# Vision tower on one core: layer norms by logarithm and exponential, folds inside the norms, pair blocks inside the last attention

## Chip, core and metric

The kernel runs on one core of a Trainium2 chip. The metric is the device time of one launch in microseconds. All data is fp32, apart from two 0/1 matrices in bf16.

## The reference

What is computed, cut to its order:

```python
h = tok(x)                          # 128 images -> 64 patches + class token, 128 wide; times pos_embed
h = h + attn0(layernorm(h))         # 8 heads; scores below the 64th best of 65 dropped;
                                    # sum over i=1..3 of gelu(alpha_i) * attn^i v
h = h + mlp0(layernorm(h))          # 64 experts' places with capacity 128, top 2, one shared MLP
h = h + attn1(layernorm(h))         # softmax attention, and a fixed distance matrix on a 4th projection
h = h + mlp1(layernorm(h))          # 8 experts, top 2 of them for each token, weights by softmax
layernorm(x) = (x - mean(x)) / sqrt(var(x) + 1e-5)      # over the 128 features
```

## The kernel before

The residual stream `h` and the normalised stream `xn` lie in SBUF whole, features on partitions, 8320 tokens in the free axis (128 images of 65). `vit_tower` (from L2202) calls one function for each stage, and each stage is a block of its own: all engines meet at its end, and each engine runs its own list of instructions in between, tied to the others by semaphores alone.

- `patch_embed` (L92) streams the images in sixteen chunks and fills `h`. ScalarE issues the small loads; GpSimd has nothing to do.
- `fold_first` (L2107) makes small folded matrices for the first attention: gelu of the alphas, their sum, `center_w` = identity - 1/128, the value weights turned on TensorE (4 transposes), scaled, and multiplied with the output weights (4 products). `fold_second` (L2167) does the like for the second layer.
- `layer_norm` (L205) is called three times (tags a0, f0, a1). It goes over 10 groups of 832 tokens. TensorE: `center` (2 matmuls of 416 columns with `center_w`, three PSUM banks in turn, L253), `variance` (four 32-row means of the squares, L260), `spread` (four matmuls that spread the inverse deviation over 128 rows into four banks, L269), in the order center(g), variance(g-1), spread(g-2). ScalarE: two copies out of PSUM (L297), square root (L289), square (L305). VectorE: reciprocal (L315) and the multiplication into `xn` (L320). The four banks of `spread` aren't doubled: spread(g) waits for normalise(g-1).
- `attention` (L394) is called twice. It goes over 64 pairs of images in a software pipeline; steps 64 to 79 are the drain. In the second call it carries `Routing` as well: for each batch of 4 tiles of 128 tokens (the sixteenth and last has 5) it turns the finished rows of `h` (`turn_rows`, L1549), computes the second norm's mean and deviation (logarithm L921, exponential L926), picks two of eight experts, ranks tokens by expert pair, and GpSimd scatters rows to the DRAM tensor `pair_rows` (`send`, L650). Before that, `complete_rows` (L637) adds the turned rows of `h` to the bias sums that TensorE made (`weigh_biases`, L1598) and ScalarE copied (`copy_biases`, L896 and L897). `normalise_rows` is L885. At the end VectorE computes a table of blocks (`find_blocks`), and SyncE clears all used semaphores in a block of its own (L1645).
- `pair_blocks` (L1895) loads 93 blocks of 128 rows from `pair_rows` (L1970), runs two experts on each (up L2010, down L2020) and scatters the results to `out` (L1990). Ahead of its first load it makes a tile of pad rows (L1985) and stores it (L1956).

## Time and profile before

| | us |
|---|---|
| three runs | 1830.36, 1833.38, 1837.22 |
| median | 1833.38 |
| profiled execution, time | 1838.73 |
| profiled execution, span from first to last instruction | 1836.9 |
| TensorE busy in the span | 1662.0 (90%) |
| VectorE, ScalarE, GpSimd busy | 1092.3, 872.8, 777.7 |

The page's picture of the span, in 40 slices of 45.9 us, digits in tenths of a slice:

```profile
## 2 busy tenths in 40 slices
PE   8999998899999999987899989999999998459997
...
PEclk9999998999999999999699989999999999679999
```

Stages by their first instruction, in us from the span's start: patches 0, first fold 268.8, norm a0 274.3, first attention 309.8, norm f0 840.9, routed MLP 876.4, second fold 1044.6, norm a1 1048.0, second attention 1081.6, semaphores cleared from 1614.1, pair blocks 1621.6, end 1836.9. A row of a timeline gives the start, the duration and, in brackets, how long the engine sat idle before it and what ended that. PE is TensorE, DVE VectorE, ACT ScalarE, POOL GpSimd, SP SyncE, and a q behind a name is that engine's sequencer. One fp32 matmul is two instructions in a row's count. The clock column is the granted TensorE clock, 1.0 for 2.4 GHz and 0.5 for 1.2 GHz.

### The profile page before, as it was taken

How to read it: one execution, taken by the hardware profiler on the slowest of the kernel's cores; microseconds unless marked ns; L12 is line 12 of the kernel's file. 1: busy time of each engine (PE TensorE's matmuls, PEld its weight loads, DVE VectorE, ACT ScalarE, POOL GpSimd, SP SyncE). 2: the span in 40 equal slices, each digit the busy share in tenths (PEclk: the TensorE clock that was granted, in tenths of full speed). 3: DMA queues.
4: the chain of work that ended last, by engine and by line, in shares of the span. 5: the costliest groups of instructions: out<-in, count | busy, mean ns of one | idle time of the engine just before them, and what ended most of it. 6: DMA issues, size and time to landing. Idle time of an engine off the chain costs nothing. (4 is left out here: it accounts for less than half of the span.)

```text
span 1836.9 us, 61849 instructions
## 1 busy us (share of the span) xinstructions
PE 1662.0 (90%) x24177; PEld 1227.1 (67%) x24177; DVE 1092.3 (59%) x3338; ACT 872.8 (48%) x2369; POOL 777.7 (42%) x925
## 2 busy tenths in 40 slices
PE   8999998899999999987899989999999998459997
PEld 3444444677777777763877647777777777358997
DVE  0000015888878888874666555766666666537765
ACT  0000006666666656545444455665656565236653
POOL 0000000788888878870011113355545454514444
PEclk9999998999999999999699989999999999679999
DMA  9877730000000000003000000000000000124422
GB/s 374 319 313 313 298 122 1 3 3 4 3 3 4 3 3 4 3 4 103 1 1 1 1 1 3 2 20 20 20 19 20 20 22 17 48 78 119 124 75 62
DMA packets 47216, 117.17 MB, mean 64 GB/s; under 512 B 10732, under 2 KB 29471, under 8 KB 46973
## 3 DMA queue, kind: packets, MB, share of 16 engines
q1 hardware_dynamic: 39198, 99.25, 15.0%
q0 software_dynamic: 6096, 12.94, 2.0%
q8 instruction: 191, 3.13, 0.7%
q10 hardware_dynamic: 1678, 1.43, 0.2%
q14 instruction: 53, 0.43, 0.1%
HBM read 96.80 MB, written 18.61 MB: 63 GB/s over the span
## 5 line engine op out<-in xcount | busy, mean ns | idle before, releaser
L1361 PE MATMUL ps<-xn,s_a_wqkv 128*128 128x260 f32 x1024 | 302.8, 414 | 29.1 <-ACT qk_a L768 22.5
L170 PE MATMUL ps<-x_chunk,s_w_tok 128*128 128x512 f32 x576 | 252.2, 599 | 6.7 <-DMA x_chunk<-in_x_main 6.7
L1361 PEld LDWEIGHTS ps<-xn,s_a_wqkv 128*128 128x128 f32 x1024 | 170.8, 192 | 105.3 <-ACT qk_a L768 71.3
L170 PEld LDWEIGHTS ps<-x_chunk,s_w_tok 128*128 128x128 f32 x576 | 109.8, 192 | 147.8 <-issue 147.8
L940 ACT ACTIVATE e_a<-e_a 128x585 f32<-128x585 f32 (+1 forms) x128 | 85.1, 665 | 167.2 <-DVE e_a L1248 96.6
L197 DVE SCALAR_TENSOR_TENSOR h<-ps,s_b_tok,s_pos 128x512 f32 (+1 forms) x16 | 11.3, 746 | 249.4 <-PE ps L178 249.4
L724 POOL TENSOR_TENSOR prob_a<-e_a,inv_sum_a 128x512 f32<-128x512 f32 x64 | 67.0, 1047 | 206.6 <-issue 111.0
L614 POOL MEMSET cls_queries_a<- 128x1040 f32 x2 | 1.9, 966 | 346.6 <-POOLq L221 346.6
L1239 DVE TENSOR_REDUCE neg_max_a<-ps 128x8 f32<-128x520 f32 x128 | 89.3, 697 | 99.1 <-PE ps L1339 99.1
L1445 PE MATMUL ps<-s_a_wqkv,xn_pair_a 128*64 128x256 f32 x1024 | 138.5, 389 | 4.5 <-ACT weightsT_m L875 2.8
L1990 POOL DMA_INDIRECT out<-block_out_m,block_m x93 | 92.1, 990 | 114.9 <-DVE block_out_m L2093 74.0
L2126 ACT ACT_TABLE_LOAD x1 | 1.3, 1283 | 268.8 <-PEq L103 268.8
L708 POOL TENSOR_TENSOR kept_a<-e_a,keep_a 128x585 f32<-128x585 f32 x64 | 87.3, 1364 | 89.8 <-issue 76.8
L1401 PE MATMUL ps<-horner_a,probT_a 64*64 64x64 f32 x2048 | 109.5, 219 | 6.0 <-issue 5.7
L1401 PE MATMUL ps<-dv_a,probT_a 64*64 64x64 f32 x2048 | 107.4, 219 | 5.8 <-issue 2.8
L768 ACT ACTIVATE qk_a<-ps 128x260 f32<-128x260 f32 x256 | 99.1, 387 | 27.9 <-PE ps L1361 19.6
L780 ACT ACTIVATE resT_a<-ps 128x260 f32<-128x260 f32 x256 | 84.5, 383 | 58.4 <-PE ps L1378 35.8
L1411 PE MATMUL ps<-probT_a,horner_a 64*64 64x65 f32 x2048 | 109.8, 224 | 1.6 <-DVE horner_a L985 1.5
L1892 POOL TENSOR_TENSOR h<-h,mlp_gated 128x320 f32<-128x320 f32 x26 | 22.4, 863 | 186.6 <-DVE mlp_gated L1872 186.6
L1411 PE MATMUL ps<-probT_a,cls_values_a 64*64 64x1 f32 x2048 | 92.1, 187 | 6.3 <-issue 6.3
L1339 PE MATMUL ps<-qk_a 64*64 64x65 f32 x4096 | 91.8, 224 | 3.4 <-issue 3.4
L1248 DVE TENSOR_TENSOR e_a<-ps,neg_max_a 128x520 f32<-128x520 f32 x128 | 89.7, 701 | 6.0
(284 smaller groups left out, 4356.5 us busy)
## 6 DMA issues: line engine op xcount, KB each, us to landing
x_chunk<-in_x_main SPq DMA_DIRECT2D x96, 768.0 KB, 8.4
block_m<-pair_rows SPq DMA_DIRECT2D x93, 130.0 KB
pair_rows<-pad_rows_m SPq DMA_DIRECT2D x29, 130.0 KB
s_f_all<-in_f_w SPq DMA_DIRECT2D x2, 1024.0 KB
x_ends<-in_x_tail SPq DMA_DIRECT2D x16, 96.0 KB, 10.7
out<-block_out_m,block_m POOLq DMA_INDIRECT x93
s_w_tok<-in_w_tok SPq DMA_DIRECT2D x6, 192.0 KB, 6.9
pair_rows<-rows_m,slot_i_m POOLq DMA_INDIRECT x65
```

Of the source, the lines that this page charges most:

```text
L170: last = nc.tensor.matmul(ps[:, bank, :], w_tok[:, k, :], xb[:, s, k, :], start=(k == 0), stop=False)
L708: nc.gpsimd.tensor_tensor(columns(kept, t.even), columns(e_of(t), t.even), columns(keep, t.even), ALU.mult).then_inc(kept_done, 1)
L768: nc.scalar.activation(qk[:, (t.j // 2) % 2, c, :], ps[:, QK_BANK[i], 0:QUAD], ACT.Identity if bias is not None else ACT.Copy, bias=bias[: ...
L940: nc.scalar.activation(columns(e_of(t), t.even), columns(e_of(t), t.even), ACT.Exp, scale=-SCALE)\
L1239: last = nc.vector.tensor_reduce(neg_max[:, :, 0:CH], score(), AX.X, ALU.min)
L1248: last = nc.vector.tensor_tensor(e_of(t)[:, :, 0:CH], score(), over_keys(neg_max[:, :, 0:CH]), ALU.subtract)
L1339: last = nc.tensor.matmul(ps[i * PATCHES:(i + 1) * PATCHES, b, c * SEQ:(c + 1) * SEQ], qk[rows, sl, c, t0 + 1:t0 + SEQ], qk[rows, sl, CH + ...
L1361: nc.tensor.matmul(ps[:, QK_BANK[i], 0:QUAD], w_qkv[:, c * P:(c + 1) * P], xn[:, t.h * QUAD:(t.h + 1) * QUAD], start=True, stop=True).then ...
L1401: last = nc.tensor.matmul(ps[rows, 2 + n, col:col + DH], pt[rows, k, c, i, 1:SEQ], values[rows, i, c, :], start=True, stop=True)
L1411: last = nc.tensor.matmul(ps[other, R_BANK[i], c * SEQ:c * SEQ + cols], values[rows, (t.j - 6) % 2, i, c, :], pt[rows, k, c, i, 0:cols], s ...
L1445: last = nc.tensor.matmul(ps[b * DH:(b + 1) * DH, V_BANK, i * CH * DH:(i + 1) * CH * DH] .rearrange("p (c d) -> p c d", c=CH), xs[:, k, i ...
L1990: nc.gpsimd.indirect_dma_start(out[:, :], bass.IndirectOffsetOnAxis(ap=blk[:, s % RB, NAME:NAME + 1].bitcast(I32), axis=0), ys[:, s % RY, ...
```

## The change

1. `layer_norm`: VectorE copies the centered values out of PSUM. ScalarE squares, then takes the logarithm of variance + eps and the exponential of -0.5 times that, which is the inverse deviation; no reciprocal is left, and the dummy square root at the head becomes an explicit choice of table set. VectorE normalises two groups behind its copies.
2. `fold_first` and `fold_second` are gone. The constants are made in `patch_embed` (ScalarE and GpSimd); the transposes and products stand in the norms' tails (`Fold`, passed to the norms a0 and a1).
3. `attention`: GpSimd runs `complete_rows` behind `add_cls`. For the last batch it isn't run; TensorE adds the rows of `h` in PSUM by five products with the identity. In the drain ScalarE normalises rows one step earlier.
4. `pair_blocks` becomes the class `PairBlocks`. Its engine parts follow the attention's in the same block, with the same instructions in the same order, and its buffers lie in `xn` and `h`. The pad rows are made at the attention's head. SyncE waits for the block table and for all scattered rows, then loads. The block that clears semaphores is left out behind the second attention.

```diff
--- before.py
+++ after.py
@@ patch_embed @@
+            nc.scalar.activation(consts.alphas[:, :, :], consts.alpha_raw, ACT.Gelu).then_inc(gelu_done, 1)
+            act.wait_ge(gelu_done, 1)
+
+        @block.gpsimd
+        def _(pool):
+            nc.gpsimd.memset(consts.mean_w[:, :], 1.0 / D).then_inc(means_set, 1)
+            nc.gpsimd.memset(consts.spread_w[:, :], 1.0 / 32).then_inc(folded, 1)
+            nc.gpsimd.memset(consts.dist_pair[:, :, :], 0.0).then_inc(folded, 1)
+            pool.wait_ge(means_set, 1)
+            pool.wait_ge(later_loaded, 16 * len(later_loads))
+            nc.gpsimd.tensor_tensor(consts.center_w[:, :], consts.ident[:, :], consts.mean_w[:, :], ALU.subtract)\
+                .then_inc(folded, 1)
+            nc.gpsimd.tensor_scalar(consts.neg_b_q[:, :], consts.b_q, -1.0, None, ALU.mult).then_inc(folded, 1)
+            pool.wait_ge(gelu_done, 1)
+            nc.gpsimd.tensor_tensor(consts.asum[:, :], consts.alphas[:, :, 0], consts.alphas[:, :, 1], ALU.add)\
+                .then_inc(asum_done, 1)
+            pool.wait_ge(asum_done, 1)
+            nc.gpsimd.tensor_tensor(consts.asum[:, :], consts.asum[:, :], consts.alphas[:, :, 2], ALU.add)\
+                .then_inc(asum_done, 1)
+            pool.wait_ge(asum_done, 2)
+            nc.gpsimd.tensor_tensor(consts.abv[:, :], consts.asum[:, :], consts.bv_col, ALU.mult).then_inc(folded, 1)
+            pool.wait_ge(folded, 5)
...
@@ layer_norm, TensorE @@
+            def turn_values():
+                pe.wait_ge(copied, 2 * groups)
+                for c in range(CH):
+                    last = nc.tensor.transpose(ps[:, 2, c * P:(c + 1) * P], fold.w_v[:, c * P:(c + 1) * P],
+                                               fold.ident[:, :])
+                last.then_inc(wvt_ps, 1)
+                for c in range(CH):
+                    last = nc.tensor.matmul(ps[:, 1, 0:fold.wide], fold.left(c), fold.right(c),
+                                            start=(c == 0), stop=(c == CH - 1))
+                last.then_inc(wide_ps, 1)
+
+            def fold_values():
+                pe.wait_ge(wvt_sb, 1)
+                for c in range(CH):
+                    last = nc.tensor.matmul(ps[:, 0, 0:D], wv_t[:, c, :], fold.w_out[:, c, :],
+                                            start=(c == 0), stop=(c == CH - 1))
+                last.then_inc(wcls_ps, 1)
+
             for g in range(groups + 2):
                 if g < groups:
                     center(g)
@@ -277,54 +337,72 @@
                     variance(g - 1)
                 if g >= 2:
                     spread(g - 2)
+                if fold and g == groups:
+                    turn_values()
+            if fold:
+                fold_values()
...
@@ layer_norm, ScalarE and VectorE @@
+            nc.scalar.preload_act_table_set("natural_log_exp_and_others")
             act.wait_ge(eps_set, 1)
-            nc.scalar.activation(warm[:, :], eps[:, :], ACT.Sqrt).then_inc(warmed, 1)
-
-            def deviation(g):
+
+            def square(g):
+                act.wait_ge(copied, 2 * g + 2)
+                since(act, var_ps, g - 1)
+                nc.scalar.activation(sq[:, g % 2], xc[:, g % SX], ACT.Square).then_inc(squared, 1)
+
+            def inverse(g):
                 act.wait_ge(var_ps, g + 1)
-                since(act, rstd_done, g - 1)
-                nc.scalar.activation(sd[:, g % 2, :], ps[:, 3, 0:n], ACT.Sqrt, bias=eps[:, 0:1])\
-                    .then_inc(sd_done, 1)
+                nc.scalar.activation(log_var[:, g % 2, :], ps[:, 3, 0:n], ACT.Ln, bias=eps[:, 0:1])\
+                    .then_inc(log_done, 1)
+                act.wait_ge(log_done, g + 1)
+                since(act, spread_ps, g - 1)
+                nc.scalar.activation(rstd[:, g % 2, :], log_var[:, g % 2, :], ACT.Exp, scale=-0.5)\
+                    .then_inc(rstd_done, 1)
 
             for g in range(groups + 1):
                 if g < groups:
-                    since(act, normed, g - SX + 1)
-                    for q in (2 * g, 2 * g + 1):
-                        act.wait_ge(center_ps, q + 1)
-                        nc.scalar.activation(xc[:, g % SX, 2 * (q % 2):2 * (q % 2) + 2, :],
-                                             ps[:, q % 3, 0:half].rearrange("p (i n) -> p i n", n=n),
-                                             ACT.Copy).then_inc(copied, 1)
+                    square(g)
                 if g >= 1:
-                    deviation(g - 1)
-                if g < groups:
-                    act.wait_ge(copied, 2 * g + 2)
-                    since(act, var_ps, g - 1)
-                    nc.scalar.activation(sq[:, g % 2], xc[:, g % SX], ACT.Square).then_inc(squared, 1)
-            act.wait_ge(warmed, 1)
+                    inverse(g - 1)
 
         @block.vector
         def _(dve):
             nc.vector.memset(eps[:, :], EPS).then_inc(eps_set, 1)
 
-            def inverse(g):
-                dve.wait_ge(sd_done, g + 1)
-                since(dve, spread_ps, g - 1)
-                nc.vector.reciprocal(rstd[:, g % 2, :], sd[:, g % 2, :]).then_inc(rstd_done, 1)
+            def copy(g):
+                since(dve, squared, g - SX + 1)
+                since(dve, normed, g - SX + 1)
+                for q in (2 * g, 2 * g + 1):
+                    dve.wait_ge(center_ps, q + 1)
+                    nc.vector.tensor_copy(xc[:, g % SX, 2 * (q % 2):2 * (q % 2) + 2, :],
+                                          ps[:, q % 3, 0:half].rearrange("p (i n) -> p i n", n=n)).then_inc(copied, 1)
 
             def normalise(g):
-                dve.wait_ge(copied, 2 * g + 2)
                 dve.wait_ge(spread_ps, g + 1)
                 nc.vector.tensor_tensor(xn[:, g * Q * n:(g + 1) * Q * n].rearrange("p (i n) -> p i n", n=n),
                                         xc[:, g % SX], ps[:, 4:4 + Q, 0:n], ALU.mult).then_inc(normed, 1)
 
-            for g in range(groups + 1):
+            for g in range(groups + 2):
                 if g < groups:
-                    inverse(g)
-                if g >= 1:
-                    normalise(g - 1)
+                    copy(g)
+                if g >= 2:
+                    normalise(g - 2)
+                if fold and g == groups:
+                    dve.wait_ge(wvt_ps, 1)
+                    turned = ps[:, 2, :].rearrange("p (c f) -> p c f", c=CH)
+                    if fold.scale is None:
+                        nc.vector.tensor_copy(wv_t[:, :, :], turned).then_inc(wvt_sb, 1)
+                    else:
+                        nc.vector.tensor_tensor(wv_t[:, :, :], turned, fold.scale.unsqueeze(2).to_broadcast([P, CH, D]),
+                                                ALU.mult).then_inc(wvt_sb, 1)
+            if fold:
+                dve.wait_ge(wide_ps, 1)
+                fold.finish(ps[:, 1, 0:fold.wide]).then_inc(wcls_sb, 1)
+                dve.wait_ge(wcls_ps, 1)
+                nc.vector.tensor_copy(fold.w_cls[:, :], ps[:, 0, 0:D]).then_inc(wcls_sb, 1)
+                dve.wait_ge(wcls_sb, 2)
...
@@ attention, SyncE and GpSimd @@
+                blocks.store_spare_rows(sp)
+                sp.wait_ge(table_done, 1)
+                for i in range(2):
+                    sp.wait_ge(sent[i], 16 * sum(route.size(k) for k in range(i, route.batches, 2)))
+                blocks.sync(sp)
...
                 k, par = at
-                n = route.size(k)
+                if isinstance(k, int) and k == LAST:
+                    return
                 upto(pool, b2_sb, k + 1, route.batches)
-                nc.gpsimd.tensor_tensor(rows[:, par, 0:n, D:2 * D], rows[:, par, 0:n, D:2 * D],
-                                        turned[:, par, 0:n, 0:D], ALU.add).then_inc(added, 1)
+                nc.gpsimd.tensor_tensor(rows[:, par, 0:route.BATCH, D:2 * D], rows[:, par, 0:route.BATCH, D:2 * D],
+                                        turned[:, par, 0:route.BATCH, 0:D], ALU.add).then_inc(added, 1)
...
+                if isinstance(k, int) and k == LAST:
+                    pool.wait_ge(b2_sb, k + 1)
+                else:
+                    upto(pool, added, k + 1, LAST)
...
@@ attention, step of GpSimd @@
-                if route and t.j % 4 == 0:
-                    complete_rows(t)
...
                 if t.even != masked and t.has(depth):
                     add_cls(t)
+                if route and t.j % 4 == 0:
+                    complete_rows(t)
...
@@ attention, ScalarE @@
+                ends = t.fixed and t.s >= pairs
                 if t.j % 4 == 0:
                     copy_turned(t, 0)
+                    if ends:
+                        normalise_rows(t)
...
@@ attention, TensorE and the end @@
                 for i in range(n):
+                    whole_rows = n > route.BATCH
                     last = nc.tensor.matmul(biases_at(i), wtt[0:n * E1, :], b2_diag[0:n * E1, i * D:(i + 1) * D],
-                                            start=True, stop=True)
+                                            start=True, stop=not whole_rows)
+                    if whole_rows:
+                        first = (k * route.BATCH + i) * P
+                        last = nc.tensor.matmul(biases_at(i), h[:, first:first + P], ident[:, :],
+                                                start=False, stop=True)
...
+                blocks.tensor(pe)
 
         stage_block.close()
+        if route:
+            return
```

## Rows read from the trace of the kernel before

**Rows 1.** Busy time by stretch: stretch, length, each engine's busy us, clock, DMA, GB/s.

```profile
1048.00:1081.60 33.60, 27.52 (x200) 12.02 (x200) 23.41 (x21) 23.39 (x42) 0.00 (x0) 0.94 0.00 1
1110.00:1555.00 445.00, 416.88 (x7061) 342.35 (x7060) 296.20 (x1001) 269.16 (x782) 214.87 (x300) 1.00 0.05 17
...
1624.80:1837.00 212.20, 189.83 (x1581) 181.09 (x1581) 141.51 (x435) 116.00 (x343) 92.08 (x93) 0.96 0.34 98
...
877.00:903.00 26.00, 26.00 (x124) 26.00 (x124) 13.75 (x68) 10.43 (x24) 0.00 (x0) 0.50 0.01 1
```

**Rows 2.** Timeline, two groups of a norm: start, duration, engine, line, operation, idle before.

```profile
1062.71 0.63 PE L269 MATMUL ps<-rstd_a,spread_w 32*128 32x208 f32 x8 [0.32 <-DVE xn L320]
...
1063.28 1.66 PE L253 MATMUL ps<-h,center_w 128*128 128x416 f32 x4
...
1064.30 0.96 DVE L320 TENSOR_TENSOR xn<-centered_a,ps 128x832 f32<-128x832 f32 x1
...
1064.87 0.56 PE L260 MATMUL ps<-squared_a,mean_w 128*32 128x208 f32 x8
...
1065.50 0.43 ACT L289 ACTIVATE deviation_a<-ps,eps_a 128x208 f32<-128x208 f32 x1
1065.83 0.89 ACT L305 ACTIVATE squared_a<-centered_a 128x832 f32<-128x832 f32 x1
1065.97 1.45 DVE L315 RECIPROCAL rstd_a<-deviation_a 128x208 f32<-128x208 f32 x1 [0.70 <-ACT deviation_a L289]
...
1065.97 1.66 PE L253 MATMUL ps<-h,center_w 128*128 128x416 f32 x4
```

**Rows 3.** Timeline, tail of the same norm: its last center and its last normalise.

```profile
1071.70 1.66 PE L253 MATMUL ps<-h,center_w 128*128 128x416 f32 x4
...
1080.31 1.02 DVE L320 TENSOR_TENSOR xn<-centered_a,ps 128x832 f32<-128x832 f32 x1 [1.35 <-PE ps L269]
```

**Rows 4.** VectorE's copies out of PSUM by line: min, median, max ns.

```profile
L1001 DVE COPY probT_a<-ps x64: 680/692/693, 1101.8 to 1568.1; 128x512 f32<-128x512 f32 x64
...
L2196 DVE COPY w_dist<-ps x1: 292/292/292, 1046.2 to 1046.2; 128x128 f32<-128x128 f32 x1
```

**Rows 5.** Timeline: both folds, the norms' first centers, the first attention's first projections.

```profile
268.83 0.63 PE L2132 MATMUL ps<-s_ident,s_a_wqkv 128*128 128x128 f32 x4 [1.92 <-PEq L103]
...
274.32 5.24 PE L253 MATMUL ps<-h,center_w 128*128 128x416 f32 x8 [0.86 <-PEq L2115]
...
311.02 6.84 PE L1361 MATMUL ps<-xn,s_a_wqkv 128*128 128x260 f32 x16 [0.46 <-ACT cls_out_a L749]
...
1044.64 0.63 PE L2179 MATMUL ps<-s_ident,s_a_wqkv 128*128 128x128 f32 x4 [1.88 <-PEq L1669]
...
1048.08 3.03 PE L253 MATMUL ps<-h,center_w 128*128 128x416 f32 x8 [0.87 <-PEq L2170]
```

**Rows 6.** Timeline, end of the last attention: rows of the last two batches.

```profile
1581.42 1.24 PE L1549 MATMUL ps<-turn_gate_m,h 128*128 128x136 f32 x4 [2.79 <-POOL h L679]
...
1592.61 2.02 ACT L885 ACTIVATE rows_m<-turned_m,row_shift_m,row_rstd_m 128x128 f32<-128x128 f32 x5
...
1594.99 2.47 PE L1598 MATMUL ps<-s_a_wqkv,weightsT_m 40*128 40x128 f32 x10 [1.66 <-issue]
...
1598.35 1.53 POOL L637 TENSOR_TENSOR rows_m<-rows_m,turned_m 128x640 f32<-128x640 f32 x1 [2.76 <-ACT rows_m L897]
...
1600.78 0.99 POOL L650 DMA_INDIRECT pair_rows<-rows_m,slot_i_m  x1 [0.90 <-POOL rows_m L637]
```

**Rows 7.** Queue drains by line (ns; first to last start); first load, last store.

```profile
L1644 POOLq DRAIN  x2: 727/3050/5374, 834.6 to 1608.6; - x2
...
L1913 POOLq DRAIN  x1: 9327/9327/9327, 1827.4 to 1827.4; - x1
...
1624.88 1.49 SPq L1970 DMA_DIRECT2D block_m<-pair_rows  x2
...
1828.06 0.98 POOL L1990 DMA_INDIRECT out<-block_out_m,block_m  x1 [0.30 <-issue]
```

More of the change, by code:

```diff
@@ L740, in _ @@
             if route:
-                for i in range(2):
-                    pool.wait_ge(sent[i], 16 * sum(route.size(k) for k in range(i, route.batches, 2)))
+                blocks.gpsimd(pool)
         @block.scalar
@@ new lines, in gpsimd @@
+    def gpsimd(self, pool):
+        nc, blk, ys, RB, RY = self.nc, self.blk, self.ys, self.RB, self.RY
+        for s in range(self.count):
+            pool.wait_ge(self.y_done, s + 1)
+            nc.gpsimd.indirect_dma_start(
+                self.out[:, :],
+                bass.IndirectOffsetOnAxis(ap=blk[:, s % RB, self.NAME:self.NAME + 1].bitcast(mybir.dt.int32), axis=0),
+                ys[:, s % RY, :], None, bounds_check=self.tokens - 1, oob_is_err=False)\
+                .then_inc(self.stored[s % RY], 16)
```

503 lines of the change are left out of this document (231 added, 272 removed).

## Prediction

> **What bounds the kernel now.** I read the page's slices first, then busy time by stretch, then the timeline at every seam. In the attention of the second layer TensorE is busy 416.9 of 445 us at the full clock, and in the pair blocks 189.8 of 212.2 us [rows 1]. There only fewer matmuls would help, and the diff removes none. What is loose lies between the stages and in the three layer norms: one norm takes 33.6 us, with TensorE busy 27.5, VectorE 23.4 and ScalarE 23.4 [rows 1]. So I cost each norm, the two fold blocks, the end of the last attention and the hole behind it.
>
> **Folds taken out of their own blocks.** The first fold runs from 268.83 to the norm's first matmul at 274.32, 5.5 us; the second from 1044.64 to 1048.08, 3.4 us [rows 5]. Both stretches go. The constants (gelu, alpha sums, center_w) move to ScalarE and GpSimd inside the patch block, which have nothing to compute for some 165 us after their loads; cover enough, and the gelu's table load is in it. What remains of a fold moves to the tail of its norm, below.
>
> **Steady part of a norm.** Groups of 832 tokens start alternately 3.04 and 2.69 us apart. The group from 1063.28 has no wait: center until 1064.87 (1.59), then variance and spread until the next center at 1065.97 (1.10), in sum 2.69; in the other the spread waits 0.32 for VectorE's normalise, which stands behind a 1.45 us reciprocal [rows 2]. After the change VectorE has two copies and the normalise. A copy of 128x512 from PSUM takes 0.69 and one of 128x128 takes 0.29, so 416 columns take about 0.59 [rows 4]: 2 x 0.59 + 0.96 = 2.14 us. ScalarE has square 0.89, logarithm and exponential. A logarithm of this shape is not in the trace; I price both like the square root, 0.43 [rows 2], so 1.75 us, against bounds of 0.2 (half of it) and 0.9 (the square) each; even at the upper bound the sum is 2.69. So TensorE sets 2.69. Seven groups from the third to the tenth go from a mean of 2.87 to 2.69, -1.2; the first variance comes some 0.3 later, as both first copies now run one behind the other ahead of the square. Net -0.9 for each of three norms. The table load at a norm's head (1.28 us) still lies beside the first centers and copies.
>
> **Tail of a norm.** From the last center (1071.70) to the end of the last normalise (1081.33) pass 9.63 us [rows 3], a chain of reciprocals and normalises through one set of PSUM banks. After: copies done at +2.3, square at +3.2, last variance at +3.9, exponential at +5.0; meanwhile the ninth normalise ends at +5.9, the last spread at +6.6, the last normalise at +7.7. That is -2.0 in the middle norm. In the outer two the fold's transposes and the four wide products stand ahead of the last spread (0.6 + 1.0 us on TensorE, 0.69 on VectorE), so it starts 0.4 later; behind it come four products, 1.1, and a copy of 0.29. I end at +8.7, -0.9 each.
>
> **Clock of the first norm.** Its first eight matmul instructions take 5.24 us, those of the second layer's norm 3.03 [rows 5]: the first stretch ran at the 1.2 GHz level, after a fold in which TensorE was mostly idle, the other at 2.4 GHz. With the fold gone TensorE goes from the patch products over a 1.9 us hole straight into centers. I take the upper level: -1.9, since filling hides part of the 2.2. The tail with its fold leaves hardly a hole ahead of the attention, whose first sixteen projection instructions took 6.84 us at the lower level [rows 5]; at the upper they could take 3.4, and as ScalarE has to empty the two banks in turn I take 4.5: -2.3, between 0 and -3.4. In the last attention a DMA of 3 us gates the start, so nothing is gained there. If the clock falls anyway, these 4.2 us are lost. The Trainium skill, page "TensorE: Matmul & The Clock Gate" (Part 1), says that the gate follows how busy the array was lately, and that it takes sustained work to get the full rate back; by that rule too the outcome hangs on the hole ahead of the norm.
>
> **Order in the last attention.** GpSimd's row sum now stands behind the class-token adds. In the loop both wait for things that come at the same times as before and GpSimd has slack, so 0. In the drain TensorE waits 2.79 us for h behind that sum [rows 6]; the next limit, ScalarE's first copy, comes 1.6 earlier than 1581.42, so 1.6 is gained. Row normalising, 2.02 us on ScalarE ahead of the last weight copy [rows 6], moves into an idle stretch in both last batches: 0.4 and 1.1. Together the last bias products start 3.1 earlier. Five more products there, at the 0.49 of one of the five now in 2.47 us [rows 6], add 2.4; GpSimd's 1.53 us sum leaves; and the first row is sent after 0.4 where it took 0.9 behind that sum [rows 6]. Sum: -3.1 + 2.4 - 1.5 - 0.4 = -2.6, give or take 1.5: the same move in the third last batch puts 1.6 us of ScalarE ahead of evictions of one step and takes it from ahead of those of the next, and I count that as nothing. VectorE's block table is ready 2 us earlier as well and isn't last.
>
> **The hole behind it.** Now: last row sent 1606.84, its landing seen by GpSimd by 1608.4, GpSimd's queue drains 5.37 us from 1608.6, then 118 semaphores are cleared until 1621.5, pads are made and stored, and the first block load issues at 1624.88 [rows 7]: 18.0 us. After: SyncE waits for the landing (1.6) and reads its row register (1.0), then loads: 2.6. So -15.4. Weight fetches of VectorE and ScalarE need only the table and lie in that wait. GpSimd's two pad memsets, 0.4 us, and the spare-row store move to the attention's head, where SyncE is idle and ScalarE waits for the iotas behind them; the 3 us DMA gates there.
>
> **A cost that comes back.** The drain isn't free elsewhere. 5.374 us for 65 indirect DMAs is 82.7 ns each. The kernel's last drain ends at 1836.7, 7.69 us after the last indirect issue ends at 1829.04, with 93 DMAs since the drain before: 82.7 ns each again [rows 7]. I take it as a cost per indirect DMA since the last drain. In one block there are 158, so 13.07 us at the end: +5.4.
>
> **Sum.** First norm: -5.5 - 0.9 - 0.9 - 1.9 - 2.3 = -11.5. Middle: -0.9 - 2.0 = -2.9. Last: -3.4 - 0.9 - 0.9 = -5.2. End of attention and hole: -2.6 - 15.4 + 5.4 = -12.6. In all -32.2 on the profiled execution of 1838.7 us (span 1836.9), so 1806.5 there. That execution lay 5.3 above the median of the runs, 1833.4; the prediction is 1801.2.
>
> **Rivals.**
> - *The drain is no more than a constant*, or cleared records are taken up while GpSimd idles: then nothing comes back. For: GpSimd is busy 92 of 212 us in the blocks [rows 1]. Against: two drains with the same 82.7. 1801.2 - 5.4 = 1796.
> - *The norms gain nothing inside*, from a latency that I don't see (copies late for the square), and the clock falls ahead of the first norm: 6.0, 2.9 and 1.8 of the three sums go, 10.7 in all: 1812.
> - *The router keeps the full clock.* Behind the middle norm TensorE runs 26 us without a hole at the lower level [rows 1]. A shorter tail might keep the upper one; then VectorE, 13.75 us of work, is next: -12, 1789. Against: TensorE is still mostly idle in that tail, which has no fold to fill it.
> - *Slower: table loads between the functions.* If square, logarithm and exponential didn't stay in one table set, each group would pay 1.28 us twice. It decides from 0.94 us on ScalarE per group (2.69 - 1.75). ScalarE's group would be 1.75 + 2.57 = 4.3, 1.6 over TensorE's, 30 times: +48.6, 1850. Against: the last attention runs logarithm and exponential at once one behind the other with identity and copy, with one load at its head. The Trainium skill ("ScalarE: Activation LUTs", Table sets) says that one named set holds exp and ln, and that cheap functions are in every set; for square this trace shows it only beside the root.
>
> **How the numbers follow.** Forecast 0.61, no drain paid again 0.12, norms flat 0.14, router at full clock 0.07, table loads 0.04, something unseen that eats most of it 0.02. The forecast's own range is 1797 to 1806 (the 4.2 us of the clock, logarithm and copy prices, 1 or 2 us in the drain). 1792 to 1812 leaves out the router, the loads and the unseen. A measurement of this kernel tells about 0.5%, 9 us, from no change: faster 0.91, same 0.05, slower 0.04.
>
> **What would show it.** Centers 2.69 apart in all three norms, with no table load between; the first eight at 3.0 us in the first norm; no TensorE instruction of a fold outside a norm; the first block load 2.6 us behind the last row's issue; no drain there, and a last drain of about 13 us behind the last store. Wrong if groups come at 2.9 or more, or if GpSimd stalls among its stores once more than 93 are out since the last drain.

## The result and the profile after

The changed kernel takes 1800.1 us (median of four runs, 1796.46 to 1800.6); the kernel before, timed beside it, 1831.9 (1824.47 to 1837.22). The ratio is 0.983, with an interval from 0.980 to 0.986: 31.8 us less, where the prediction had 32.2 less and 1801.2. A second comparison, with both kernels timed on one chip, gave 1815.2 against 1847.1, 0.985 (0.982 to 0.987), again 31.9 less. The number was right. Its terms were not all: one cost that I added hardly exists, and another, of about the same size, I did not see.

The first rows are busy time by stretch of the changed kernel's first profiled execution (time 1796.46 us, span 1794.6): stretch, its length, busy us and instructions of TensorE, of its weight loads, of VectorE, ScalarE and GpSimd, then the granted clock, the DMA share and GB/s. They are the first norm, the router, the middle of the last attention and the pair blocks.

```profile
268.00:299.10 31.10, 28.92 (x220) 13.96 (x221) 22.60 (x34) 17.35 (x31) 0.03 (x1) 1.00 0.01 2
866.00:894.00 28.00, 27.89 (x131) 27.92 (x132) 14.88 (x74) 9.17 (x23) 0.00 (x0) 0.50 0.00 1
1110.00:1555.00 445.00, 413.08 (x7049) 341.71 (x7048) 305.56 (x1070) 270.25 (x791) 222.96 (x306) 1.00 0.05 18
1582.00:1794.60 212.60, 190.46 (x1581) 181.38 (x1581) 141.15 (x435) 115.56 (x343) 92.89 (x93) 0.96 0.34 98
```

Beside [rows 1]: a norm with its fold inside now takes 31.1 us, with TensorE busy 28.9 of them; a norm alone took 33.6 with 27.5. The router is still at 0.50, that is 1.2 GHz, and the two long stages are what they were.

One whole group of the middle norm, from the timeline (start, duration, engine, line, operation, idle time before):

```profile
850.06 1.67 PE L295 MATMUL ps<-h,center_w 128*128 128x416 f32 x4
850.20 1.02 DVE L384 TENSOR_TENSOR xn<-centered_f,ps 128x832 f32<-128x832 f32 x1 [0.49 <-PE ps L311]
...
850.54 0.42 ACT L357 ACTIVATE log_variance_f<-ps,eps_f 128x208 f32<-128x208 f32 x1
...
850.99 0.38 ACT L361 ACTIVATE rstd_f<-log_variance_f 128x208 f32<-128x208 f32 x1
851.16 1.19 DVE L379 COPY centered_f<-ps 128x416 f32<-128x416 f32 x2
...
851.65 0.56 PE L302 MATMUL ps<-squared_f,mean_w 128*32 128x208 f32 x8
...
852.14 0.63 PE L311 MATMUL ps<-rstd_f,spread_w 32*128 32x208 f32 x8
852.39 0.90 ACT L353 ACTIVATE squared_f<-centered_f 128x832 f32<-128x832 f32 x1 [1.02 <-DVE centered_f L379]
...
852.71 1.66 PE L295 MATMUL ps<-h,center_w 128*128 128x416 f32 x4
```

Centers come 2.65 apart, group after group, with no waiting TensorE; [rows 2] had 2.69 and 3.04 in turn. VectorE works 2.21 and ScalarE 1.70 of the 2.65. No table load stands between square, logarithm and exponential: with that the slower rival falls. The Trainium skill ("ScalarE: Activation LUTs", Table sets) says that one set has logarithm and exponential together; the trace agrees, and shows square under that set too, with one load of 1.28 us at each norm's head.

The seams of the same execution. TensorE at the first norm's head, in its folded tail and at the attention's start:

```profile
268.05 3.03 PE L295 MATMUL ps<-h,center_w 128*128 128x416 f32 x8 [1.93 <-PEq L111]
...
297.07 1.16 PE L329 MATMUL ps<-s_a_wout,wvT_a 128*128 128x128 f32 x8
...
300.24 3.69 PE L1457 MATMUL ps<-xn,s_a_wqkv 128*128 128x260 f32 x12 [0.46 <-ACT cls_out_a L837]
...
304.30 1.14 PE L1457 MATMUL ps<-xn,s_a_wqkv 128*128 128x260 f32 x4 [0.36 <-ACT qk_a L856]
```

The first eight center instructions take 3.03 where [rows 5] had 5.24, and the sixteen projections are through after 5.2 us where they took 6.84. Last come the old hole and the end: the last row's issue, the first block load, the first product behind it, the last store, and the queue drains by line (min/median/max ns, first to last start).

```profile
1578.49 0.96 POOL L739 DMA_INDIRECT pair_rows<-rows_m,slot_i_m  x1 [0.30 <-issue]
...
1581.99 1.48 SPq L2090 DMA_DIRECT2D xn<-pair_rows  x2
...
1584.03 0.48 PE L2119 MATMUL ps<-s_ident,xn 128*128 128x128 f32 x1 [11.66 <-DMA xn<-pair_rows]
...
1785.32 0.98 POOL L2106 DMA_INDIRECT out<-h,xn  x1 [0.31 <-issue]
...
L1746 POOLq DRAIN  x2: 728/5235/9742, 827.8 to 1784.6; - x2
```

From the end of the last row's issue (1579.45) to the load are 2.5 us; in [rows 7] there are 18.0. The last drain ends at 1794.39, 8.08 behind the last store's issue (1786.31), where it was 7.66 before.

Reading such seams off ten of the profiled executions gives this table, in us; the columns are the two profiles of either kernel and one of each experiment that follows. The stages run from the last patch product to the first scores, from there to the last class-token add, from the middle norm's first matmul to the router's, on to the last expert add, to the second attention's first scores, through 64 steps to the last pair's probabilities, to the last row's issue, to the first block load, to the last store's issue, and to the end.

| | before, second profile | order only | changed, first profile | order back | before, first profile | norms only | folds out | own block | changed, second profile | eight small matmuls |
|---|---|---|---|---|---|---|---|---|---|---|
| first norm with fold | 53.9 | 53.9 | 40.5 | 41.5 | 52.1 | 50.6 | 50.6 | 40.5 | 40.5 | 41.6 |
| first attention | 518.5 | 522.0 | 522.5 | 525.0 | 516.8 | 518.2 | 520.6 | 522.3 | 525.2 | 524.8 |
| middle norm | 35.0 | 35.0 | 31.9 | 31.9 | 35.5 | 31.9 | 32.3 | 31.9 | 31.9 | 32.0 |
| router, experts | 169.6 | 169.6 | 169.7 | 169.7 | 167.9 | 169.6 | 169.6 | 169.8 | 169.8 | 156.7 |
| fold, last norm | 49.4 | 48.5 | 42.9 | 42.9 | 48.9 | 45.8 | 45.1 | 42.8 | 42.9 | 42.6 |
| last attention | 459.5 | 459.5 | 459.4 | 459.5 | 469.0 | 469.2 | 469.0 | 468.9 | 468.8 | 469.0 |
| its end | 44.8 | 42.9 | 41.3 | 43.2 | 44.7 | 44.9 | 45.9 | 44.5 | 44.5 | 44.6 |
| hole | 18.2 | 18.5 | 2.5 | 2.5 | 18.0 | 18.0 | 2.5 | 8.3 | 2.5 | 2.6 |
| pair blocks | 206.2 | 199.8 | 204.4 | 205.8 | 204.2 | 205.1 | 208.5 | 202.3 | 205.0 | 202.9 |
| last drain | 7.9 | 7.9 | 8.3 | 8.3 | 7.9 | 7.9 | 8.3 | 7.9 | 8.3 | 8.3 |
| span | 1833.6 | 1828.0 | 1794.6 | 1801.9 | 1836.9 | 1831.7 | 1823.1 | 1810.4 | 1810.0 | 1796.9 |

The reader is to see two families in the row of the last attention: 459.4 to 459.5, and 468.8 to 469.2, whatever the kernel. The two profiles that I compared first lie in different ones. That gives a span difference of 42.3 us, of which 9.6 has nothing to do with the change. Within one family the spans differ by 39.0 and 26.9 us, on either side of the 32 of the timed runs, so single executions scatter by several us. From the stage differences I had expected 40 us and a ratio of 0.978 for the second comparison; it gave 0.985.

### The profile page after: what moved, and what is told of

It reads as the page before. It is cut to its first block and busy times, and to the rows that moved or that the text cites. A ratio compares the mean times of both kernels' runs of the same rounds, so it can differ in the third digit from the quotient of the medians.

```text
span 1794.6 us, 61648 instructions
## 1 busy us (share of the span) xinstructions
PE 1654.6 (92%) x24187; PEld 1223.5 (68%) x24187; DVE 1083.3 (60%) x3361; ACT 849.9 (47%) x2334; POOL 778.0 (43%) x932
## 3 DMA queue, kind: packets, MB, share of 16 engines
q8 instruction: 191, 3.13, 0.7%
## 5 line engine op out<-in xcount | busy, mean ns | idle before, releaser
L2106 POOL DMA_INDIRECT out<-h,xn x93 | 92.9, 999 | 114.0 <-DVE h L2219 107.4
L1541 PEld LDWEIGHTS ps<-s_a_wqkv,xn_pair_a 128*64 128x64 f32 x1024 | 67.5, 137 | 36.4 <-issue 17.2
```

The source lines that it names most:

```text
L1541: last = nc.tensor.matmul(ps[b * DH:(b + 1) * DH, V_BANK, i * CH * DH:(i + 1) * CH * DH] .rearrange("p (c d) -> p c d", c=CH), xs[:, k, i ...
L2106: nc.gpsimd.indirect_dma_start(self.out[:, :], bass.IndirectOffsetOnAxis(ap=blk[:, s % RB, self.NAME:self.NAME + 1].bitcast(mybir.dt.int32 ...
```

## The experiments

**The kernel before once more, and the order of GpSimd's row sum.** On that first comparison the last attention had become 9.6 us shorter, in steps of 0.8 per period of four pairs, and the only edit in its loop is the order of two things on GpSimd. Either that order costs 0.8 per period (theory A), or it is something of the execution (theory B, TensorE's instruction supply). I ran the kernel before again, the changed kernel with the order undone, and the kernel before with that edit alone. The edit, as in the second of them:

```diff
             def step(t):
+                if route and t.j % 4 == 0:
+                    complete_rows(t)
                 if t.has(1):
...
                 if t.even != masked and t.has(depth):
                     add_cls(t)
-                if route and t.j % 4 == 0:
-                    complete_rows(t)
```

> The kernel before, unchanged, so that a second profiled execution of it stands beside the first. The first one was at 1838.7 us, above all timed runs (1824.5 to 1837.2). In the last attention, whose four-pair period is 31.2 us there and 30.4 after the change, each theory says what a second look shows. Theory A (the order of GpSimd's row sum costs 0.8 us per period, 12 times): the period is 31.2 again, since the order is in the program. Theory B (TensorE's instruction supply ran dry once per period in that one execution): the period can be 30.4 here, and the span some 9 us shorter. The ratio to the kernel before is 1.000 by both.

> The changed kernel with one edit: in the last attention's loop GpSimd's row sum stands ahead of the class-token adds again, as before. TensorE's program is untouched. Theory A (that order cost 12 x 0.8 us in the loop, besides 1.6 in the drain): the period goes from 30.4 to 31.2 us and the whole time from 1800 to some 1811. My forecast's reading (GpSimd has slack in the loop, the order counts in the drain alone): 1801 to 1802, period 30.4. Theory B (instruction supply of TensorE): same as the forecast's reading.

> The kernel before with that one edit of the change: GpSimd's row sum behind the class-token adds. Theory A: 1832 less 11 = 1821. The forecast's reading: 1832 less 1.6 at the most, 1830. Theory B: no change beyond the scatter of the kernel before.

Measured: 1830.2 against 1829.5 for the kernel before (ratio 1.000), 1803.6 for the order undone (0.986, 0.983 to 0.988), 1827.4 for the order alone (1.000, 0.998 to 1.003). The last attention takes 459.5 in all three: theory A is wrong. The order counts only at the attention's end, where both kernels show 1.9 us: 44.8 to 42.9 with the edit alone, 41.3 to 43.2 with it undone, against 1.6 in the forecast. In the timeline of GpSimd with the order alone, the row sum of the third last batch now stands behind the add that it used to hold up:

```profile
1572.56 0.73 POOL L679 TENSOR_TENSOR h<-h,cls_terms_a 128x260 f32<-128x260 f32 x1 [4.07 <-DVE h L1020]
1574.66 1.26 POOL L637 TENSOR_TENSOR rows_m<-rows_m,turned_m 128x512 f32<-128x512 f32 x1 [1.37 <-ACT rows_m L897]
```

1.9 us is a tenth of a per cent, too little for whole runs to tell; only the seams show it. Theory B holds no better as it stands. The slow loops appeared in every kernel of two later sets of runs, each set on one chip, and in none of this one. So the family goes with the chip that a set runs on, or with something else of its time; the runs don't tell which. From 1200 to 1500 us TensorE is idle on "issue" for 3.2 us in the first profile of the kernel before and for none in the second; that is less than half of the 0.8 us in each of some ten periods, and what the rest is stays open.

**What a drain of GpSimd's queue costs.** The last drain was to be 13.07 us and is 8.08 behind the last issue. A kernel with nothing but row scatters measures the law by itself. Its body, once for each count:

```diff
+        with nc.Block() as sixty_five:
+            @sixty_five.gpsimd
+            def _(pool):
+                send_rows(nc, pool, region, rows, place, sems[3], 42, 65)
```

> Leaves out the whole model: the output is zeros. GpSimd alone sends rows to DRAM by indirect DMAs of 128 rows of 1040 bytes, as the last attention does, 2, 8, 32, 65, 158 and three times 65 of them, each batch in a block of its own, so that GpSimd's queue drains at each end; each DMA waits for the landing of the one two before it. In the sixth batch GpSimd waits for the last landing before the block ends, in the seventh it then idles some 20 us more, in the eighth it computes some 5 us between two DMAs. The forecast's rule (82.7 ns for each indirect DMA since the last drain): 0.2, 0.7, 2.6, 5.4, 13.1, 5.4, 5.4 and 5.4 us. Rival (a constant after the last issue, some 7 to 8 us less what has passed by the drain's start, whatever the count): about 7 in the first five, 5 in the sixth, near 0 in the seventh, 7 in the eighth. A third reading (cost by the number of DMAs up to a limit, or of those not yet taken up): 158 at once gives far more than 8, and the slow eighth batch gives less than the fourth.

The drains of the batches, by line, as above, without the second:

```profile
L89 POOLq DRAIN  x1: 3893/3893/3893, 26.1 to 26.1; - x1
...
L97 POOLq DRAIN  x1: 4181/4181/4181, 89.2 to 89.2; - x1
L101 POOLq DRAIN  x1: 6556/6556/6556, 189.5 to 189.5; - x1
L105 POOLq DRAIN  x1: 5004/5004/5004, 428.3 to 428.3; - x1
L109 POOLq DRAIN  x1: 5352/5352/5352, 531.2 to 531.2; - x1
L114 POOLq DRAIN  x1: 5350/5350/5350, 659.2 to 659.2; - x1
L125 POOLq DRAIN  x1: 5346/5346/5346, 942.6 to 942.6; - x1
```

Where the drain follows at once, its record opens 1.2 us before the last DMA has been issued, so the first five hold that issue too. From the last issue's end the five end after 1.7, 1.9, 3.0, 5.4 and 3.8 us. The last three, 65 DMAs each, cost 5.35 whether GpSimd had waited for the landing, idled 24 us more or computed between the DMAs: the second rival, a constant that passes while one waits, is wrong, and 82.3 ns for each DMA is right up to 65. But 158 cost less than 65. So I asked for more counts, each batch landed before its block ended.

> Leaves out the whole model: the output is zeros. GpSimd sends 48, 80, 93, 110, 126, 142, 158 and 200 times 128 rows, each batch in a block of its own, and waits for the last landing before the block ends. The first such run gave a drain of 82 ns for each of 8 to 65 DMAs but only 3.8 us behind 158. If the cost stays at a plateau above 65: 3.9, then 5.35 throughout, less for 158. If finished DMAs are taken up in bulk once a ring is full: rising with 82 ns each, 3.9, 6.6, 7.7, 9.1, up to some count and then back to a small value, as a saw's tooth.

```profile
L89 POOLq DRAIN  x1: 3973/3973/3973, 98.7 to 98.7; - x1
L94 POOLq DRAIN  x1: 6581/6581/6581, 226.0 to 226.0; - x1
L99 POOLq DRAIN  x1: 7637/7637/7637, 372.8 to 372.8; - x1
L104 POOLq DRAIN  x1: 9021/9021/9021, 549.9 to 549.9; - x1
L109 POOLq DRAIN  x1: 1185/1185/1185, 751.4 to 751.4; - x1
L114 POOLq DRAIN  x1: 2487/2487/2487, 967.7 to 967.7; - x1
L119 POOLq DRAIN  x1: 3798/3798/3798, 1209.7 to 1209.7; - x1
L124 POOLq DRAIN  x1: 7224/7224/7224, 1518.7 to 1518.7; - x1
```

These are 48, 80, 93, 110, 126, 142, 158 and 200 DMAs. The first four cost 82 to 83 ns each. The others cost as much as 14, 30, 46 and 88 would (1185 / 14 = 85, 7224 / 88 = 82): 112 fewer. A saw's tooth, then. And in each of the last four batches one step stands out: the 114th DMA starts 2.6 to 3.4 us after the 113th, where a step takes 1.5. So 112 finished DMAs are taken up there at once, for 1 to 2 us, where a drain would pay 9.2 for them.

The changed kernel does the same. Its 158 DMAs since the last drain are 65 rows and 93 stores. In both of its profiled executions one store, the 50th, comes some 0.9 us later behind its data than the others (1.63 and 1.72 against 0.79). In the first of them it is the one at 1698.07:

```profile
1698.07 0.98 POOL L2106 DMA_INDIRECT out<-h,xn  x1 [0.30 <-issue]
1699.52 1.15 POOL L2106 DMA_INDIRECT out<-h,xn  x1 [0.46 <-issue]
```

It is the 115th DMA since the drain before. The five other kernels here in which rows and stores share a block have the same store late, 1.34 to 1.61 us behind its data; where a drain stands between them (own block, the norms alone, the kernel before) it comes after 0.79. At 82.3 ns each the drain at the end pays for 8.08 / 0.0823 = 98, so by this estimate 60 had been taken up. Why 60 here and 112 there, with stores of another form among them, stays open.

**The pair blocks in a block of their own.** The changed kernel with that part undone, but for the clearing of semaphores and the early pads:

```diff
...
         stage_block.close()
         if route:
+            with nc.Block() as pair_block:
+                pair_block.sync(blocks.sync)
+                pair_block.gpsimd(blocks.gpsimd)
+                pair_block.tensor(blocks.tensor)
+                pair_block.scalar(blocks.scalar)
+                pair_block.vector(blocks.vector)
             return
```

> The changed kernel with the pair blocks in a block of their own again, but with no semaphores cleared between and the pads already made: of the old hole only the leaving and entering of a block is back, with GpSimd's queue drain of 65 indirect DMAs. From the last row's issue to the first block load: landing 1.6 to 1.8, drain 5.37, barrier and reading of a register some 1.5, so 8.5 to 9 where the changed kernel has 2.5 and the kernel before 18.2. The rest of the old hole, 9.5, is then the clearing of 118 semaphores and the pads. At the end my forecast's rule said that the drain of the changed kernel would be 5.4 longer than that of this one; its profile shows 8.08 us after the last store's issue, so here 7.66 as in the kernel before: 0.4 less. In all 1800 + 5.8 = 1806. If the drain were only moved (the forecast's rule), it would be 1800.

Measured: 1814.0 against 1845.6 (0.984, 0.981 to 0.986). The queue drain of the seam, the second of this line, and the first load behind it:

```profile
L1741 POOLq DRAIN  x2: 719/3046/5374, 827.6 to 1593.6; - x2
...
1600.22 1.49 SPq L2091 DMA_DIRECT2D xn<-pair_rows  x2
```

The hole is 8.3 us where the changed kernel has 2.5, and the last drain ends 7.66 behind the last store's issue, not 8.08. So of the 15.5 us that the change takes out of the hole, the block's border with its drain is 5.8, and the clearing and the pads, the rest, are 9.7. Of the 5.8, 0.4 is paid later. Whole runs don't show these 5.4 us (the changed kernel's own ratio is no smaller, 0.985): here the pair blocks took 2.7 less than in the changed kernel's second profile, and over the ten executions they vary from 199.8 to 208.5.

**The norms alone, and the folds taken out.** One kernel is the one before with the new inside of the norms, the other the changed one with both folds in blocks of their own again:

```diff
-        layer_norm(nc, "a0", tokens, h, xn, ps, center_w, mean_w, spread_w, fold=first_fold)
+        fold_first(nc, ps, mean_w, S["ident"], S["a0_wqkv"][:, 2 * INNER:3 * INNER], S["a0_alpha_col"][:, :, :],
...
+        layer_norm(nc, "a0", tokens, h, xn, ps, center_w, mean_w, spread_w)
```

> The kernel before with one part of the change: the inside of the layer norms (logarithm and exponential on ScalarE, copies on VectorE), no fold in them, everything else as before. My forecast's terms: 0.9 in the steady part and 2.0 in the tail of each norm, 2.9 three times, 8.7 in all; so the stretch from the middle norm's first matmul to the router's goes from 35.0 or 35.5 to 32.4, and the time from 1829.5 to 1821. Rival (the norms gain nothing inside, the gain of the changed kernel there came from the clock and the folds): 1829, and 35 us for the middle norm. The clock of the first norm's first eight matmuls stays at the lower level in both, since the fold block still stands ahead of it: 5.24 us.

> The changed kernel with the folds taken back out into blocks of their own, as before. Forecast's terms undone: the two blocks 5.5 and 3.4, the clock of the first norm and of the attention's start 1.9 and 2.3, less 1.1 twice for the fold in the tails: 10.9 in all, from 1800 to 1811; the first eight centers at 5.24 us again where the changed kernel has 3.03, the first sixteen projections at 6.8 where it has 4.8. Rival (the clock fell before for another reason than the fold block, and stays up now because of the shorter tail): the eight centers at 3.03, 1807.

Measured: 0.9955 (0.9938 to 0.9972) for the norms alone, 8.3 us (5 to 11 by the interval) of the 8.7 forecast; 0.988 (0.985 to 0.990) with the folds out. In the table the middle norm goes from 35.0 or 35.5 to 31.9 by its inside alone. TensorE at the first seam with the folds out:

```profile
267.51 0.63 PE L238 MATMUL ps<-s_ident,s_a_wqkv 128*128 128x128 f32 x4 [1.92 <-PEq L111]
...
274.03 5.86 PE L367 MATMUL ps<-h,center_w 128*128 128x416 f32 x8 [0.86 <-PEq L221]
```

The fold's idle stretch is back, and the centers behind it run at the lower level again: 5.86 us for what takes 3.03. The first sixteen projections take 6.98 us, where the changed kernel has 5.2. So the rival that the shorter tail alone had kept the clock is wrong. From the last patch product to the first scores the folds cost 10.1 us (50.6 against 40.5), and around the last norm 2.2 (45.1 against 42.9). The Trainium skill ("TensorE: Matmul & The Clock Gate", Part 1) says that the gate follows how busy the array was lately; the trace agrees, with 5.86 us behind the fold's idle stretch and 3.03 behind a hole of 1.93. Of these 12.3 us the first attention gives 4.6 back (520.6 against 525.2). In whole runs I had expected the folds to cost 10.9 us; the timed runs show some 6 (0.988 against the changed kernel's 0.985), with intervals that overlap.

**The clock behind the middle norm.** The rival at 1789 said that the router might keep the full clock. It didn't; this run asks whether it could. Matmuls that nobody reads fill the tail of the middle norm:

```diff
+            def keep_busy(count):
+                for _ in range(count):
+                    nc.tensor.matmul(ps[:, 2, 0:half], center_w[:, :], h[:, 0:half], start=True, stop=True)
...
+                if not fold and g == groups:
+                    pe.wait_ge(copied, 2 * groups)
+                    keep_busy(2)
...
```

> The changed kernel with nine more matmuls in the middle norm alone, 128x416 into a bank that nobody reads: two ahead of the last variance, three ahead of the last spread, four behind it, all where TensorE waits in the changed kernel. Nothing else changes. It tests the rival that gave 1789 in my prediction (the router behind the middle norm at the full clock). If filling the tail's holes keeps the clock at the upper level, the router's 28 us at 0.50 shrink to VectorE's 15 or so: 1800 - 12 = 1788. If the router's own small matmuls let the clock fall, or the holes were not the cause: 1800 to 1801, with the clock at 0.50 through the router as before.

Measured: 1802.2 against 1845.6, 0.977 (0.975 to 0.979). The filling itself is too long (the middle norm takes 35.4 us), but router and experts fall from 169.8 to 156.9. The next run cuts it to 208 columns and eight matmuls, to fit the holes:

> The changed kernel with eight small matmuls more in the middle norm alone, 128x208 into a bank that nobody reads: two ahead of the last variance, three ahead of the last spread, three behind it. The larger ones of the run before cost 3.5 us themselves and brought 12.8 in the router; these are cut to fit the holes of 0.97, 1.24 and 1.38 us. If a matmul of 208 columns is 0.35 to 0.4 us, the norm grows by 0.5 at most, and the router and the experts behind it take 157 us where they took 169.7: 12 us less than the changed kernel. If the smaller filling doesn't keep the clock up, 0 to 1 us more than the changed kernel.

Measured: 1799.8 against 1847.1, 0.976 (0.973 to 0.978), beside the changed kernel's 0.985 (0.982 to 0.987) in the same set: 15 us less than the change. The seams account for 13 (156.7 against 169.8, and 0.1 more in the norm), where 12 were expected. The router's stretch and the clock in it, as the first rows above:

```profile
870.00:898.00 28.00, 24.26 (x169) 21.30 (x170) 23.54 (x117) 15.60 (x35) 0.00 (x0) 0.94 0.01 1
```

TensorE is granted 0.94 where it had 0.50. VectorE is busy 23.5 of 28 us where it had 14.9: in the changed kernel's 28 us, at 0.50, it waited 12.3 us, in twelve pieces, for the router's logits, and here it waits 1.6 for them.

> The same, with twelve such matmuls more while the semaphores are cleared ahead of the middle norm (5 us in which TensorE idles; its first eight centers then took 4.52 us where 3.03 is the time at the upper level), and twelve more in the wait ahead of the first pair block (11.7 us idle; the first two products there took 1.92 and 1.31 us where later ones take 1.06). If the filling keeps or brings the clock up: 1.5 and some 1 us less than the run with the middle norm's tail alone. If it comes too late for the clock: nothing, and no loss, as long as the twelve end before the first block's load lands, 0.7 us each at the lower level.

Measured: 1799.1, 0.975 (0.973 to 0.977), no different from the run before. The seams say that the first filling does what it should (the middle norm takes 30.6 instead of 32.0) and the second little (the pair blocks 202.3 instead of 202.9), but the first attention took 2.3 us longer and router and experts 1.2, and that eats both. Of these kernels the one with eight matmuls is the version to keep: it beats both kernels of the case.

## Why the prediction was right, and where it wasn't

Measured against the steps, from the seams of the four profiles of the two kernels as they are; where two numbers stand, the first pairs the second profile of before with the first of the change, the other pairs the remaining two.

- *First norm, -11.5*: -13.4 and -11.6. The folds make 10.1 of it where I had 8.6 (5.5 + 1.9 + 2.3 - 1.1). The clock went as forecast in both pairs, with 3.03 us for the centers and 5.2 for the projections, which I had put at 4.5. For the projections that isn't sure: with the order undone and in the three kernels with fillings, whose program is the same up to there, they took 6.25 to 6.5 us, part of it at the lower level, behind centers of 3.03.
- *Middle norm, -2.9*: -3.1 and -3.6. The mechanism is the one described; the group is 2.65, not 2.69, and the tail 7.8, where I had 7.7.
- *Fold and last norm, -5.2*: -6.5 and -6.0, with the fold at 2.2 (I had 3.4 - 1.1 = 2.3).
- *End of the attention, -2.6, give or take 1.5*: -3.5 and -0.2. The order's share is 1.9 (I had 1.6). What made the second pair differ isn't shown, but the granted clock goes with it: 0.66 over this stage in the change's first profile, 0.60 in its second (0.61 and 0.62 before). The lower level holds for 27.6 us of the first and 34.2 of the second; at half speed the 6.6 us between them are worth up to 3.3, by estimate, and the stages differ by 3.2. In every profile of the other family the changed end takes 44.4 us or more (45.9 with the folds out). Beside it GpSimd waited 4.7 us for VectorE's `h` ahead of a class-token add in the second and 1.9 in the first. The two stretches, in the form of [rows 1]:

```profile
1538.00:1579.50 41.50, 23.12 (x179) 18.37 (x178) 25.23 (x141) 11.27 (x34) 24.12 (x26) 0.66 0.15 53
```

```profile
1553.90:1598.40 44.50, 21.30 (x151) 16.52 (x140) 22.49 (x128) 11.33 (x34) 20.46 (x22) 0.60 0.14 50
```

- *Hole, -15.4*: -15.7 and -15.5.
- *Drain comes back, +5.4*: +0.4. This is the step that failed. It took "a cost per indirect DMA since the last drain" from two drains, of 65 and 93 DMAs (the second is 7.66 us long, not 7.69, so 82.4 ns each). Both lie on the rising side of a tooth that falls back at some 113. Nothing in the trace of before had a count above 93, so the sum went by a line drawn on past its last point. I had written that a stall among the stores once more than 93 are out would prove it wrong: that stall is the store at 1698.07. The rival at 1796, with its chance of 0.12, came nearer: records are taken up before the end, though not while GpSimd idles (24 us of idling took up none) but when it issues the next.
- *The first attention, not in the sum*: +4.0 and +8.4. The diff doesn't touch its code. Without the drain's return my sum is 37.2 and the time 1796; 4 to 8 us here bring it back to 1800 to 1804. The two errors cancel, and that is luck.

What is known of the last point. The kernels with the folds inside the norms all have 522 to 525 us there (527 with the second filling); the kernel before has 516.8 and 518.5, the norms alone 518.2, the folds out 520.6. But the order alone has 522.0, and the code of its first attention, and of all that stands ahead, is that of the kernel before. So the same code varies by 5.2 us between executions, which is as much as there is to explain: the seven profiles with the changed code ahead have 524.3 on the mean, the three with the old code 519.1.

Part of it is the granted clock. TensorE runs at the lower level for none of the stage in both profiles of before and in that of the norms alone, and is busy 480.6 to 481.2 us there; in the nine other profiles, that of the order alone among them, it runs there for 3 to 7 us and is busy 482.5 to 485.2. The stage's last eight output products, the eight matmuls of these rows, show it, first in the kernel before (first profile), then with the order alone; after the change they take 3.66 and 3.68:

```profile
832.00:834.10 2.10, 1.99 (x8) 1.44 (x8) 0.03 (x1) 0.00 (x0) 0.00 (x0) 1.00 0.03 8
```

```profile
835.90:839.70 3.80, 3.61 (x8) 2.31 (x8) 0.07 (x1) 0.00 (x0) 0.00 (x0) 0.55 0.02 4
```

Most of TensorE's idle time in the stage is put to "issue", waiting for nothing that the profile shows (engine, line, releaser, us in total, times, longest). First the norms alone, then the changed kernel's second profile:

```profile
PE ps L1440 <- issue: 9.7, 10, 1.6
PE ps L1450 <- issue: 6.7, 6, 1.6
```

```profile
PE ps L1497 <- issue: 9.6, 10, 1.5
PE ps L1507 <- issue: 9.6, 9, 1.6
```

All lines together are idle on issue for 20.5 and 22.1 us in the two profiles of before, 22.5 and 24.8 in those of the change. But the norms alone have 22.5 too, in a stage of 518.2. Of the 4.0 us of the first pair, 3.0 are time in which TensorE is busy and 0.4 are issue; of the 8.4 of the second, 2.5 and 4.3. That the stage was longer in both pairs is measured. How much of it the change causes is not shown, nor that it does so through the place of its code: no run moved the code alone.

So the right total rests on the norms and the hole, which were read from the right rows, and on two errors of some 5 us with opposite signs, of which the second may be in part an accident of the executions. The remaining rival, table loads between the functions, and the one in which the norms gain nothing are both ruled out, by the group above and by the norms alone.

## What to carry over

Compare stage by stage, on executions of one set, before you compare whole spans: 9.6 of the 42 us between my first two profiles belonged to the execution, and an edit of the loop stood ready as a false explanation. A law taken from two points of a trace holds between them; if the change goes past them, both ends belong in the sum as cases. And where a stage that TensorE bounds runs at half the clock behind a short tail, fill the tail: eight small matmuls that nobody reads brought 13 us, some 40% of what the whole change brings.

## What I had not expected of the hardware

A drain of GpSimd's queue costs 82 ns for each indirect DMA not yet taken up (5.35 us for 65), even 24 us after the last of them has landed, and in the runs with row scatters alone GpSimd takes them up by itself in one go of 1 to 2 us when the 114th is issued. The drain after 110 such DMAs costs 9.0 us, after 126 it costs 1.2.

TensorE's straight-line program isn't free. In the first attention it stops some fifteen times, for about 1 us each, ahead of a small matmul that waits for no semaphore. The longest in the first profile of the change:

```profile
413.88 0.28 PE L1497 MATMUL ps<-horner_a,probT_a 64*64 64x64 f32 x3
415.97 0.27 PE L1497 MATMUL ps<-horner_a,probT_a 64*64 64x64 f32 x2 [1.82 <-issue]
```

The page lists an instruction queue with 191 packets, 3.13 MB in all, so 16 KB each, beside 24,187 matmuls and as many weight loads. That is 253 of these instructions to a packet. In the stretch that ends with this stop TensorE began 148 matmuls and 138 weight loads within 2.15 us of work, more than a packet's worth:

```profile
412.00:415.90 3.90, 2.15 (x148) 2.07 (x138) 3.30 (x14) 0.75 (x2) 2.79 (x4) 1.00 0.01 4
```

One packet starts at 413.6, 2.4 us ahead of the stop's end, and over the first attention a packet starts every 5 us. All 15 stops of this kind (those over 0.2 us), 15.9 us in sum, end between 2.3 and 2.7 us behind the start of a packet (in the second profile of before 19 of 19, also 15.9 us, between 2.2 and 2.9). That fits an engine that outruns its own code: 14 to 18 of some 520 us, in every kernel of this study. Whether a loop would avoid the stops was not tried. The Trainium skill ("Runtime: NRT & Kernel Launch", Instruction fetch mechanics) says that code is streamed in blocks of 16 KiB over the engine's own DMA queue and that this is hidden because the sequencer dispatches slower than the blocks come. The trace agrees on the blocks and not on the hiding: in the first attention, where one instruction follows another every 20 ns on the mean and every 8 in the stretch above, some 16 us of 520 are lost to it, if the stops are what they seem.
